# Layer 0 of a four-layer graph network: the pad term goes to one lane of four, and GpSimd clears the other three

## The chip, the core and the metric

The kernel runs on one core of a Trainium2 chip. The metric is the device time of one execution in microseconds (us), compared as a median of runs.

## The reference, cut to what matters

Four graph layers run over 128 graphs of 128 nodes with 64 features. Only layer 0 is touched. `F` is 64 and the hidden width `H` is 192.

```python
h = jnp.maximum(_layernorm(x, axis=-1), 0.0)
mask = (adj > 0.0).astype(x.dtype)
xj_proj = h @ W1a
diff = h[:, :, None, :] - h[:, None, :, :]
e = jax.nn.relu(xj_proj[:, :, None, :] + diff @ W1b + b1)
hm = jnp.einsum('bjkh,bjk->bjh', e, mask)
deg = jnp.sum(mask, axis=-1)
x = x + hm @ W2 + deg[..., None] * b2
```

For each node, a relu of (a term of the node) + (a term of the neighbour) is summed over the node's neighbours, and the sum goes through `W2`.

## The kernel before, in words

The rewritten sum needs two rows per node, made by one product per graph (`pe_ac`, L509): `A`, the node's own term, and `C`, the neighbour's. ScalarE copies them out as `ac32` (float32, L690) and `ac_hi` (float16, L691), and GpSimd makes the rest `ac_lo = ac32 - ac_hi` (`pool_low`, L883).

A node's neighbours are gathered slot by slot. In each of 8 slots of a chunk, a one-hot matrix (VectorE, `dve_onehot`, L811) picks one neighbour for every node, and TensorE adds the picked `C` row to the seeded `A` row in a PSUM bank (`pe_half`, `pe_next_half`, L551). Four slots are a half, 128 x 768 numbers wide. VectorE takes the negative part of each half and adds it to `acc`, a sum with four lanes of 192 (`dve_half`, L829). Later chunks do not start again: VectorE subtracts the old one-hot from the new one (`dve_difference`, L823) and TensorE adds that difference. In the trace each graph has two chunks, so four executions of L829. Nodes with many neighbours keep three more shared slots (`dve_shared_onehot`, L817, for the one-hot; `act_shared`, L708, to cut them).

Empty slots of a node add a known amount. That is the pad term, a relu of `A` times a negative factor `neg_pad` (per node, L781). `act_pads` (L699) starts `acc` with it: it writes a quarter of the term to each of the four lanes, so that VectorE's first L829 can add to it. After the last L829 of a graph, GpSimd folds the lanes, first four to two (`pool_sum`, L897), then the shared slots (L899, L901), and TensorE transposes and adds what is left (`pe_transpose_sum`, L523 to L528).

All five engines walk the same 128 steps, one graph a step, each with its own instruction order written out by hand and semaphores between them. A group is four steps, here called q = 0 to 3, and the preparation of the next group is spread over them: in q = 1 VectorE works out slot counts (L745 to L781), in q = 2 the first rows (L786 to L794), in q = 3 `dve_past_last` (L799, four instructions) and `dve_host_rows` (L805), for which `pe_host_ranks` (L494) waits. `acc`, `ac32`, `ac_hi` and `ac_lo` have four buffers, one for each q.

In step b, VectorE first waits for `s_acc0` (the start value of `acc`), then loops over the later chunks (one here), then does the two last halves with L817 between them. GpSimd in the same step, as soon as L823 is done, folds the graph before (L897, L899, L901), then makes `ac_lo` of the graph two ahead (L883), and then waits for the next L823:

```python
def step(b, g, u, q, nxt, p, use):
    if not (known(b) and b + 2 >= B):
        pool_low(pool, b + 2, (q + 2) % GS)
    pool_sum(pool, b, g, q, total, first)
```

ScalarE in step b cuts the shared slots of graph b - 1 (L708), seeds the second half of graph b (L715), copies `A` and `C` of graph b + 2 (L690, L691), and writes the start value of graph b + 1 (L699).

Of the kernel before, what the change touches and what calls it, by code (L numbers as in the profile page):

```python
# [7 lines left out]
ALU = mybir.AluOpType  # L8
ACT = mybir.ActivationFunctionType
# [3 lines left out]
def gnn_stack_kernel(nc, a, out):  # L13
# [12 lines left out]
    B, N, F = a["x"].shape  # L26
    H = a["L0_gnn_W2"].shape[0]
    D1 = a["L1_gnn_W0"].shape[1]
    GS = 4
    NG = B // GS  # L30
    NI = NG // 2
    SU = 4
    SC = 2 * SU
    SS = 3
# [14 lines left out]
    with ctx:  # L49
        def sb(name, shape, dt=F32):  # L50
            return ctx.enter_context(nc.sbuf_tensor(name, shape, dt))

        def sem(name):
            return ctx.enter_context(nc.semaphore(name))
# [94 lines left out]
        pad = sb("pad", [N, GS])  # L149
# [4 lines left out]
        neg_pad = sb("neg_pad", [N, 2, GS])  # L154
        h0 = sb("h0", [N, GS * F])
        hT0 = sb("hT0", [F + 1, 2, GS * N])
        ac32 = sb("ac32", [N, 4, 2 * H])
        ac_hi = sb("ac_hi", [N, 4, 2 * H], F16)
        ac_lo = sb("ac_lo", [N, 4, 2 * H], F16)
        acc = sb("acc", [N, 4, SU * H])  # L160
# [235 lines left out]
        s_rows = sem("rows_per_candidate_made")  # L396
        s_sum = sem("rows_per_candidate_summed")
        s_nop = sem("slot_count_step")
        s_n = sem("slot_counts_ready")
        s_st = sem("first_host_rows_made")  # L400
        s_first = sem("first_host_rows_copied")
# [23 lines left out]
        s_T = sem("sum_transposed")  # L425
# [13 lines left out]
        def known(v):  # L439
            return isinstance(v, int)  # L440
# [174 lines left out]
        def all_iterations(eng, body, prefetch_back_edge=False):  # L615
            around(0, body)
            with nc.Fori(1, NI - 1, engines=bass.OrderedEngineSet([eng.engine]),
                         hint_back_edge=prefetch_back_edge) as i:
                around(i, body)
            around(NI - 1, body)  # L620

        def group_of(b, g, u, q, back):

            r = q - back
            if 0 <= r < GS:
                return g, u, r
            return (g - 1, 1 - u, r + GS) if r < 0 else (g + 1, 1 - u, r - GS)
# [65 lines left out]
        def act_pads(act, b, g, p, q):  # L693

            act.wait_ge(s_n, g + 1)
            act.wait_ge(s_hi, b + 1)
            if not (known(b) and b < 4):
                act.wait_ge(s_hm, b - 3)
            nc.scalar.activation(acc[:, q, :].rearrange("p (t h) -> p t h", t=SU),  # L699
                                 ac32[:, q, 0:H].unsqueeze(1).broadcast_to([N, SU, H]), ACT.Relu,  # L700
                                 scale=neg_pad[:, p, q:q + 1]).then_inc(s_acc0, 1)

        def act_shared(act, b, q):
# [64 lines left out]
        def dve_pieces(dve, g, p):  # L768

            v = nc.vector  # L770
            dve.wait_ge(s_nop, 12 * g + 8)
            v.tensor_scalar(left_i[:, :], left[:, :], float(SS - 1), float(DIV), ALU.max, ALU.mult).then_inc(s_nop, 1)
            dve.wait_ge(s_nop, 12 * g + 9)
            v.tensor_scalar(pieces_i[:, :], left_i[:, :], SH, None, ALU.arith_shift_right).then_inc(s_nop, 1)
            dve.wait_ge(s_nop, 12 * g + 10)
            v.tensor_copy(pieces[:, :], pieces_i[:, :])
            v.scalar_tensor_tensor(out=pad[:, :], in0=pieces_i[:, :], scalar=-float(SS), in1=left[:, :],
                                   op0=ALU.mult, op1=ALU.add).then_inc(s_nop, 1)
            dve.wait_ge(s_nop, 12 * g + 11)

            v.tensor_scalar(neg_pad[:, p, :], pad[:, :], -float(SS - 1), 1.0 / SU, ALU.add, ALU.mult).then_inc(s_n, 1)  # L781

        def dve_first_rows(dve, g, p):
            dve.wait_ge(s_st, g + 1)
# [22 lines left out]
        def dve_onehot(dve, ranks, key, pos):  # L807

            dve.reg_alu(pos, pos, CH, ALU.bitwise_xor)
            at = dve.snap(pos, min_val=0, max_val=CH)  # L810
            nc.vector.tensor_scalar(onehot[:, ds(at, CH)], ranks.rearrange("p t j -> p (t j)"),  # L811
                                    slot_key[:, ds(key, 1)], None, ALU.is_equal).then_inc(s_G, 1)

        def dve_shared_onehot(dve, g, u, q):

            dve.wait_ge(s_rs2, g + 1)
            nc.vector.tensor_scalar(onehot2, rs2[:, u, q, :, :].rearrange("p t j -> p (t j)"),  # L817
                                    slot_key[:, 0:1], None, ALU.is_equal).then_inc(s_G2, 1)

        def dve_difference(dve, pos, old):  # L820

            at, at_old = (dve.snap(r, min_val=0, max_val=CH) for r in (pos, old))
            nc.vector.tensor_tensor(onediff[:, ds(at, CH)], onehot[:, ds(at, CH)], onehot[:, ds(at_old, CH)],  # L823
                                    ALU.subtract).then_inc(s_D, 1)

        def dve_half(k, q):

            sums = acc[:, q, :].rearrange("p (t h) -> p t h", t=SU)
            nc.vector.scalar_tensor_tensor(out=sums, in0=unit((q + k) % 2, 0, SU), scalar=0.0, in1=sums,  # L829
                                           op0=ALU.min, op1=ALU.add).then_inc(s_free[k], 1)  # L830

        def dve_slots(dve, b, g, u, q, regs, halfway, middle, beside, summed, late):
            cnt, prev, pos, old, count_reg = regs
            n = dve.snap(count_reg, min_val=1, max_val=NC + 1)
            dve.wait_ge(s_acc0, b + 1)
            dve.reg_mov(prev, cnt)
            dve.reg_add(cnt, cnt, 1)
            with dve.Fori(0, n) as c:
                dve.reg_mov(old, pos)
                dve_onehot(dve, rs[:, u, q, :, :], c + 1, pos)  # L840
                dve.reg_mov(prev, cnt)
                dve.reg_add(cnt, cnt, 1)
                dve.wait_ge(s_G, cnt)
                dve_difference(dve, pos, old)
                dve.wait_ge(s_done[0], prev)
                dve_half(0, q)
                dve.wait_ge(s_done[1], prev)
                dve.wait_ge(s_free[0], prev)
                dve_half(1, q)
            if not (known(b) and b == B - 1):  # L850
                g1, p1, q1 = group_of(b, g, u, q, -1)
                dve.wait_ge(s_n, g1 + 1)
                dve.reg_load(count_reg, chunks[0:1, ds(b + 1, 1)])
            halfway()
            dve.wait_ge(s_done[0], cnt)
            dve.wait_ge(s_free[1], prev)
            dve_half(0, q)
            middle()
            dve_shared_onehot(dve, g, u, q)
            beside()  # L860
            dve.wait_ge(s_done[1], cnt)
            dve.wait_ge(s_free[0], cnt)
            dve_half(1, q)
            summed()
            if not (known(b) and b == B - 1):
                dve.wait_ge(s_rs, g1 + 1)
                dve_onehot(dve, rs[:, p1, q1, :, :], 0, pos)
            late()
# [12 lines left out]
        def pool_low(pool, b, q):  # L881
            pool.wait_ge(s_hi, b + 1)
            nc.gpsimd.tensor_tensor(ac_lo[:, q, :], ac32[:, q, :], ac_hi[:, q, :], ALU.subtract)\  # L883
              .then_inc(s_lo, 1)

        def pool_sum(pool, b, g, q, total, first):
            pool.wait_ge(s_n, g + 1)
            n = pool.value_load(chunks[0:1, ds(b, 1)], min_val=1, max_val=NC + 1)
            pool.reg_add(total, total, n)
            pool.wait_ge(s_free2, b + 1)  # L890
            if not (known(b) and b == B - 1):
                pool.reg_add(first, total, 1)
                pool.wait_ge(s_D, first)
            else:
                pool.reg_add(first, total, B)
                pool.wait_ge(s_free[1], first)
            nc.gpsimd.tensor_tensor(acc[:, q, 0:2 * H], acc[:, q, 0:2 * H], acc[:, q, 2 * H:4 * H], ALU.add)  # L897
            shared = acc2[:, q % 2, :]
            nc.gpsimd.tensor_tensor(shared[:, 0:H], shared[:, 0:H], shared[:, H:2 * H], ALU.add).then_inc(s_half, 1)  # L899
            pool.wait_ge(s_half, b + 1)  # L900
            nc.gpsimd.tensor_tensor(hm2[:, q % 2, 0:H], shared[:, 0:H], shared[:, 2 * H:3 * H], ALU.add).then_inc(s_hm, 1)  # L901

        with nc.Block() as block:
# [179 lines left out]
            @block.gpsimd  # L1083
            def _(pool):
                total = pool.alloc_register("pool_differences")
                first = pool.alloc_register("pool_next_difference")
                pool.reg_mov(total, 0)
                pool_low(pool, 0, 0)
                pool_low(pool, 1, 1)

                def step(b, g, u, q, nxt, p, use):
                    if not (known(b) and b + 2 >= B):
                        pool_low(pool, b + 2, (q + 2) % GS)
                    pool_sum(pool, b, g, q, total, first)

                all_iterations(pool, step)
# [604 lines left out]
```

## Time and profile before

| | |
|---|---|
| median of 3 runs | 1501.34 us (1501.23 to 1503.02) |
| the profiled execution | 1501.28 us |
| its span, first to last instruction | 1499.6 us |
| mean granted TensorE clock | 0.968 |
| TensorE matmul busy | 1331.5 us (89%) |
| VectorE busy | 1172.1 us (78%) |
| ScalarE busy | 1112.1 us (74%) |
| GpSimd busy | 495.7 us (33%) |

The shares are averages over four layers with different limits. Layer 0 runs from about 52 us to 1034 us of the span, so what the change does is read from that stage.

### The profile page before, as it was taken

To read this page: it belongs to the slowest core of one execution; us is meant where nothing else is said; L and a number is where in the kernel's file an instruction comes from. 1 tells how busy PE (TensorE), PEld (TensorE's weight loads), DVE (VectorE), ACT (ScalarE), POOL (GpSimd) and SP (SyncE) were. 2 spreads that over 40 slices of the span, in tenths; PEclk is the share of its full clock that TensorE was granted. 3 is DMA by queue.
4 is the path that set the end of the run, shared out by engine and by line. 5 is a ranking of instruction groups with operands and counts; after the bars stand their busy time and mean duration, and the time that the engine had idled before them with its cause. 6 is when DMAs were issued, how large, how long until landed. Compare 5 with 4: busy or idle time off the path is not lost. (4 is left out here: it accounts for less than half of the span.)

```text
span 1499.6 us, 41694 instructions
## 1 busy us (share of the span) xinstructions
PE 1331.5 (89%) x11307; PEld 1084.8 (72%) x11308; DVE 1172.1 (78%) x3088; ACT 1112.1 (74%) x2424; POOL 495.7 (33%) x611
## 2 busy tenths in 40 slices
PE   0799999999999999999999999997999997881498
PEld 0577777777777777777777777775889987810498
DVE  6598898988988889889898898885444446968655
ACT  0788888888888888888888888873555555726675
POOL 0143344444444334333444444432111110076300
PEclk9999999999999999999999999998999998976699
DMA  7000000000000000000000000000000000000022
GB/s 148 15 9 9 15 7 7 7 14 7 7 7 10 11 7 7 7 14 7 7 7 14 7 7 7 0 2 1 1 0 0 0 0 0 0 1 0 11 49 52
DMA packets 40749, 18.08 MB, mean 12 GB/s; under 512 B 19396, under 2 KB 40710, under 8 KB 40710
## 3 DMA queue, kind: packets, MB, share of 16 engines
q1 hardware_dynamic: 40178, 17.39, 4.7%
q8 instruction: 19, 0.31, 0.1%
q10 hardware_dynamic: 532, 0.21, 0.1%
q14 instruction: 20, 0.16, 0.0%
HBM read 13.40 MB, written 4.19 MB: 12 GB/s over the span
## 5 line engine op out<-in xcount | busy, mean ns | idle before, releaser
L829 DVE SCALAR_TENSOR_TENSOR acc<-slot_banks,acc 128x768 f32<-128x768 f32 x512 | 486.8, 951 | 44.0 <-PE slot_banks L551 34.0
L897 POOL TENSOR_TENSOR acc<-acc 128x384 f32<-128x384 f32 x128 | 128.1, 1001 | 565.4 <-DVE onediff L823 560.9
L551 PE MATMUL slot_banks<-ac_hi,work 128*128 128x192 f16 x1408 | 264.4, 246 | 1.0 <-ACT slot_banks L715 1.0
L551 PE MATMUL slot_banks<-ac_lo,work 128*128 128x192 f16 x1408 | 263.9, 246 | 0.0
L551 PE MATMUL slot_banks<-ac_hi,onediff 128*128 128x192 f16 x1024 | 186.9, 248 | 20.8 <-DVE acc L829 16.9
L551 PE MATMUL slot_banks<-ac_lo,onediff 128*128 128x192 f16 x1024 | 185.8, 246 | 0.0
L551 PEld LDWEIGHTS slot_banks<-ac_hi,work 128*128 (+1 forms) x1408 | 137.3, 98 | 62.5 <-issue 43.4
L551 PEld LDWEIGHTS slot_banks<-ac_lo,work 128*128 (+1 forms) x1408 | 138.0, 98 | 14.9 <-issue 6.3
L811 DVE TENSOR_SCALAR work<-work,slot_key 128x1024 f16 x256 | 119.6, 478 | 28.6 <-issue 28.6
L551 PEld LDWEIGHTS slot_banks<-ac_hi,onediff 128*128 x1024 | 104.2, 102 | 43.2 <-issue 39.8
L708 ACT ACTIVATE work<-slot_banks 128x576 f32<-128x576 f32 x128 | 83.2, 650 | 68.6 <-PE slot_banks L551 68.6
L883 POOL TENSOR_TENSOR ac_lo<-ac,ac_hi 128x384 f16<-128x384 f32 x128 | 117.3, 916 | 48.1 <-ACT ac_hi L691 48.1
L651 ACT ACTIVATE work<-bank 128x512 f16<-128x512 f32 x256 | 130.5, 601 | 0.0
L699 ACT ACTIVATE acc<-ac,neg_pad 128x768 f32<-128x768 f32 x128 | 119.3, 932 | 0.0
L509 PE MATMUL bank<-wac,hT 65*128 65x384 f32 x256 | 109.2, 509 | 4.1 <-ACT ac_hi L691 4.1
L715 ACT ACTIVATE slot_banks<-ac 128x768 f32<-128x768 f32 x127 | 103.5, 815 | 11.6
L823 DVE TENSOR_TENSOR onediff<-work x128 | 88.6, 692 | 24.5 <-DVE work L811 24.5
L551 PEld LDWEIGHTS slot_banks<-ac_lo,onediff 128*128 x1024 | 100.7, 98 | 0.0
L1204 POOL TENSOR_TENSOR adjT_all<-adjT_all,ident 128x512 f32 x32 | 39.9, 1268 | 173.1 <-PE slot_banks L1158 173.1
L1125 ACT ACTIVATE onediff<-x_all,nmr,rstd 128x64 f32 (+1 forms) x256 | 90.6, 429 | 7.7 <-PE slot_banks L1295 3.2
L544 PE MATMUL slot_banks<-ac_hi,ident 128*128 128x384 f16 x258 | 84.6, 328 | 9.0 <-issue 7.8
L266 DVE BATCH_NORM_STATS2 bn<-x_all 128x6 f32<-128x64 f32 (+1 forms) x512 | 83.9, 212 | 8.0 <-DMA x_all<-in_x_dram 7.5
(254 smaller groups left out, 3330.3 us busy)
## 6 DMA issues: line engine op xcount, KB each, us to landing
adj_in<-in_adj_dram SPq DMA_DIRECT2D x32, 256.0 KB, 2.8
out_dram<-acc SPq DMA_DIRECT2D x32, 128.0 KB, 2.0
l1w<-in_L_gnn_W_dram SPq DMA_DIRECT2D x2, 64.0 KB
l1b<-in_L_gnn_b_dram SPq DMA_DIRECT2D x2, 64.0 KB
x_all<-in_x_dram SPq DMA_DIRECT2D x4, 0.2 KB, 12.0
nm_in<-in_nodemask_dram ACTq DMA_DIRECT2D x1, 64.0 KB
w1a<-in_L_gnn_W_dram ACTq DMA_DIRECT2D x1, 48.0 KB
w1b<-in_L_gnn_W_dram ACTq DMA_DIRECT2D x1, 48.0 KB
```

The source lines that it names most:

```text
L509: nc.tensor.matmul(pAC[:, 0:2 * H], hT0[:, p, q * N:(q + 1) * N], wac[:, :], start=True, stop=True)\
L544: nc.tensor.matmul(unit(pair, t, n), node, part[:, q, 0:H].unsqueeze(1).broadcast_to([N, n, H]), start=(e == 0), stop=False)
L551: last = nc.tensor.matmul(unit(pair, t, 1), hot(t), part[:, q, H:2 * H].unsqueeze(1), start=False, stop=(e == 1 and (t % SB == SB - 1 or t ...
L651: last = nc.scalar.activation(rs[:, p, :, t, :], pA3[:, :].rearrange("p (q j) -> p q j", q=GS), ACT.Copy, bias=-float(t))
L699: nc.scalar.activation(acc[:, q, :].rearrange("p (t h) -> p t h", t=SU), ac32[:, q, 0:H].unsqueeze(1).broadcast_to([N, SU, H]), ACT.Relu, ...
L715: nc.scalar.activation(unit((q + 1) % 2, 0, SU), ac32[:, q, 0:H].unsqueeze(1).broadcast_to([N, SU, H]), ACT.Copy).then_inc(s_seed, 1)
L811: nc.vector.tensor_scalar(onehot[:, ds(at, CH)], ranks.rearrange("p t j -> p (t j)"), slot_key[:, ds(key, 1)], None, ALU.is_equal).then_in ...
L823: nc.vector.tensor_tensor(onediff[:, ds(at, CH)], onehot[:, ds(at, CH)], onehot[:, ds(at_old, CH)], ALU.subtract).then_inc(s_D, 1)
L829: nc.vector.scalar_tensor_tensor(out=sums, in0=unit((q + k) % 2, 0, SU), scalar=0.0, in1=sums, op0=ALU.min, op1=ALU.add).then_inc(s_free[k ...
L883: nc.gpsimd.tensor_tensor(ac_lo[:, q, :], ac32[:, q, :], ac_hi[:, q, :], ALU.subtract)\
L897: nc.gpsimd.tensor_tensor(acc[:, q, 0:2 * H], acc[:, q, 0:2 * H], acc[:, q, 2 * H:4 * H], ALU.add)
L1125: ins = nc.scalar.activation(hn[:, u, SLOT[q] * F:(SLOT[q] + 1) * F], x[:, ds((b + q) * F, F)], ACT.Relu, bias=nmr[:, ds(b + q, 1)], scale ...
```

## The change

ScalarE's L699 writes the whole pad term to lane 0 alone, 128 x 192 numbers in place of 128 x 768, and `neg_pad` loses its factor of a quarter. GpSimd sets the three other lanes to zero with a new memset (`pool_clear`), one for each graph, placed behind `pool_low` in GpSimd's step. GpSimd first waits until the sum that last used the buffer was transposed, and VectorE waits for the memset (`s_zero`) beside `s_acc0`.

```diff
@@ act_pads
-            nc.scalar.activation(acc[:, q, :].rearrange("p (t h) -> p t h", t=SU),
-                                 ac32[:, q, 0:H].unsqueeze(1).broadcast_to([N, SU, H]), ACT.Relu,
+            nc.scalar.activation(acc[:, q, 0:H], ac32[:, q, 0:H], ACT.Relu,
                                  scale=neg_pad[:, p, q:q + 1]).then_inc(s_acc0, 1)
@@ dve_pieces
-            v.tensor_scalar(neg_pad[:, p, :], pad[:, :], -float(SS - 1), 1.0 / SU, ALU.add, ALU.mult).then_inc(s_n, 1)
+            v.tensor_scalar(neg_pad[:, p, :], pad[:, :], -float(SS - 1), None, ALU.add).then_inc(s_n, 1)
@@ dve_slots
             dve.wait_ge(s_acc0, b + 1)
+            dve.wait_ge(s_zero, b + 1)
@@ new
+        def pool_clear(q):
+
+            nc.gpsimd.memset(acc[:, q, H:SU * H], 0.0).then_inc(s_zero, 1)
@@ gpsimd
                 pool.reg_mov(total, 0)
+                pool_clear(0)
                 pool_low(pool, 0, 0)
...
                 def step(b, g, u, q, nxt, p, use):
+                    if not (known(b) and (b < 3 or b + 1 >= B)):
+                        pool.wait_ge(s_T, b - 2)
                     if not (known(b) and b + 2 >= B):
                         pool_low(pool, b + 2, (q + 2) % GS)
+                    if not (known(b) and b + 1 >= B):
+                        pool_clear((q + 1) % GS)
                     pool_sum(pool, b, g, q, total, first)
```

## Rows read from the trace of the kernel before

**Rows 1.** One stretch: us, busy PE PEld DVE ACT POOL (count), clock, DMA.
```profile
100.00:1000.00 900.00, 866.22 (x7925) 699.09 (x7923) 803.41 (x1980) 774.95 (x1590) 357.38 (x472) 1.00 0.03 8
```

**Rows 2.** Who waited for whom, 100 to 1000 us: total, times, longest.
```profile
ACT work L708 <- PE slot_banks L551: 63.3, 117, 1.0
DVE acc L829 <- PE slot_banks L551: 27.0, 75, 0.7
PE slot_banks L551 <- DVE acc L829: 16.3, 31, 2.5
PEld slot_banks L544 <- DVE acc L829: 15.3, 29, 0.8
PEld bank L494 <- issue: 7.0, 29, 0.3
```

**Rows 3.** Instructions of VectorE in order of time: start, length, idle before.
```profile
403.70 0.31 DVE L817 TENSOR_SCALAR work<-work,slot_key 128x384 f16<-128x384 f16 x1
...
406.66 0.48 DVE L811 TENSOR_SCALAR work<-work,slot_key 128x1024 f16 x1 [0.41 <-issue]
...
411.22 0.31 DVE L817 TENSOR_SCALAR work<-work,slot_key 128x384 f16<-128x384 f16 x1
...
412.71 0.73 DVE L794 TENSOR_SCALAR host<-row,start 128x128 f16<-128x128 f16 x4
...
415.77 0.96 DVE L829 SCALAR_TENSOR_TENSOR acc<-slot_banks,acc 128x768 f32<-128x768 f32 x1 [0.19 <-PE slot_banks L551]
...
418.33 0.40 DVE L805 TENSOR_TENSOR host<-host,work 128x512 f16<-128x512 f16 x1
418.65 0.94 DVE L829 SCALAR_TENSOR_TENSOR acc<-slot_banks,acc 128x768 f32<-128x768 f32 x1
```

**Rows 4.** TensorE in order of time, in the same two steps.
```profile
409.15 0.25 PE L551 MATMUL slot_banks<-ac_hi,onediff 128*128 128x192 f16 x1 [0.46 <-DVE acc L829]
...
418.83 0.38 PE L494 MATMUL bank<-row_slots,ones 128*128 128x512 f16 x1
...
419.74 0.32 PE L544 MATMUL slot_banks<-ac_hi,host 128*128 128x384 f16 x1
```

**Rows 5.** Groups by line, 100 to 1000 us: busy, mean ns of one, idle before.
```profile
L699 ACT ACTIVATE acc<-ac,neg_pad 128x768 f32<-128x768 f32 x118 | 110.0, 932 | 0.0
L720 ACT ACTIVATE hmTa<-bank,unscale 128x128 f32<-128x128 f32 x119 | 43.7, 367 | 12.9 <-PE bank L528 12.5
L799 DVE TENSOR_SCALAR work<-row,end 128x128 f16<-128x128 f16 x120 | 45.5, 439 | 0.0
L794 DVE TENSOR_SCALAR host<-row,start 128x128 f16<-128x128 f16 x120 | 22.0, 246 | 0.0
L817 DVE TENSOR_SCALAR work<-work,slot_key 128x384 f16<-128x384 f16 x117 | 36.0, 308 | 0.0
```

**Rows 6.** GpSimd's memsets, whole span: busy, mean ns of one.
```profile
L1199 POOL MEMSET onediff<- 128x896 f32 x1 | 0.8, 845 | 0.0
...
L298 POOL MEMSET hm<- 128x128 f32 x1 | 0.2, 204 | 0.0
```

**Rows 7.** VectorE and GpSimd around L799 in one q = 3 step.
```profile
417.00 0.95 DVE L799 TENSOR_SCALAR work<-row,end 128x128 f16<-128x128 f16 x1
...
416.98 0.91 POOL L883 TENSOR_TENSOR ac_lo<-ac,ac_hi 128x384 f16<-128x384 f32 x1
```

**Rows 8.** GpSimd in order of time, q = 1 and q = 2 of that group.
```profile
402.74 0.92 POOL L883 TENSOR_TENSOR ac_lo<-ac,ac_hi 128x384 f16<-128x384 f32 x1
408.11 1.00 POOL L897 TENSOR_TENSOR acc<-acc 128x384 f32<-128x384 f32 x1 [4.45 <-DVE onediff L823]
...
410.29 0.91 POOL L883 TENSOR_TENSOR ac_lo<-ac,ac_hi 128x384 f16<-128x384 f32 x1
```

**Rows 9.** VectorE's register and semaphore instructions, 400 to 432 us: ns min/median/max.
```profile
L834 DVEq FUSED_REGOPS  x3: 51/58/58, 406.1 to 429.1; - x3
...
L856 DVEq EVENT_SEMAPHORE  x4: 21/21/21, 402.5 to 425.7; - x4
```

More of the change, by code:

```diff
@@ L398, in gnn_stack_kernel @@
         s_nop = sem("slot_count_step")
+        s_zero = sem("sum_lanes_cleared")
         s_n = sem("slot_counts_ready")
```

## The prediction, written before the change was run

> **What bounds the kernel now.** I read the table of stretches first. In 900 us of layer 0, TensorE is busy for 866, VectorE for 803, ScalarE for 775 and GpSimd for 357 [rows 1]. So two engines are near their limit, and the change takes work from a third. Whether that third one ever holds anybody up is told by the list of waits: ScalarE's L708 stands idle 117 times for TensorE, 63.3 us in all, nearly once in each of the 118 steps there [rows 2]. So ScalarE is early in every step, and no wait for its start value (L699) is in the list. TensorE and VectorE wait for each other instead: VectorE's L829 for gathers, 27.0 us, TensorE's L551 and L544 for L829, 16.3 and 15.3 us [rows 2].
>
> Then I read the order of time, to see which of the two leads in which step. In q = 1 VectorE runs from L817 at 403.70 to L811 at 406.66 without idling for TensorE; only in front of that L811 stand 0.41 us in which it handles register and wait instructions [rows 3]. TensorE is behind it there: at 409.15 it has waited 0.46 us for L829 [rows 4]. In q = 2 the lead passes to TensorE: L829 at 415.77 has waited 0.19 us for it [rows 3]. In q = 3 it comes back: L805 ends at 418.73 and TensorE's L494, which needs it, starts at 418.83; L829 ends at 419.59 and L544, which needs that, starts at 419.74 [rows 3, 4]; TensorE's weight loads stood idle before L494 in 29 groups, 7.0 us [rows 2]. So a delay of VectorE in q = 1 or q = 3 is a delay of the whole group, and one in q = 2 is one beyond the first 0.19 us.
>
> **Removed: three quarters of L699.** It takes 932 ns for 768 columns; the nearest small ScalarE row, 128 columns, takes 367 [rows 5]. On the line between them 192 columns are about 0.42 us, an estimate, so about 0.51 us of each step goes, 65 us of ScalarE's time over 128 steps. On the path it gives nothing: L708 waits for TensorE afterwards as it did before, only longer [rows 2]. The dropped factor in L781 changes the operation's constants and not its shape of 128x4: nothing.
>
> **Added on GpSimd: one memset a step.** 128 columns took 204 ns, 896 took 845 [rows 6], so 576 columns are 204 + 448 x 0.835 = 578 ns. Its place is right behind L883. GpSimd then has time: it stands idle 4.45 us before the next L897 [rows 8]; were that cover gone, each step's fold would be 0.58 us later. Its own wait, for a transpose of two steps earlier, is met long before; behind it stand L883, the memset and the next fold, all inside that idle time. The result is in time for VectorE as well: behind the L883 that ends at 411.20 [rows 8] it is there at about 411.8, and VectorE first writes that buffer behind the L794 that start at 412.71 [rows 3].
>
> **Added on VectorE: one more wait a step.** The nearest rows are 21 ns for a semaphore instruction and 51 to 58 for one of registers [rows 9]. I take 0.07 us, bounds 0.02 and 0.14. It is hidden wherever VectorE's queue runs ahead of its datapath, and exposed where the 0.41 us gap stands, which is in front of two of four steps, one of them in [rows 3]: 0.14 us a group.
>
> **What the memset meets: the main term.** L799 and L794 are the same operation on the same shape, yet L799 takes 439 ns in the mean and L794 246 [rows 5]. The order of time shows why [rows 7]: one L799 starts at 417.00, beside GpSimd's L883, which started at 416.98, and both end together, L883 at 417.89 and L799 at 417.95. So this kind of VectorE instruction (TENSOR_SCALAR, float16, SBUF to SBUF) stands still while a GpSimd instruction that began before it runs. L817 and L811 are of that kind. L817 now never pays: its mean is 308 ns [rows 5], since it follows L883's end by a hair, 403.70 after 403.66 and 411.22 after 411.20 [rows 3, 8]. The memset fills exactly that place.
>
> The Trainium skill, SBUF — State Buffer, section Who interferes with whom, says that VectorE in a two-port mode and GpSimd lock each other out of a shared port pair for a whole instruction. By that rule the sum is the one below; [rows 7] agree for a GpSimd instruction that reads and writes, and no row of this trace shows it for a memset, which only writes.
>
> How much, in us, with the memset until 0.54 after L883's end (0.58 less the 0.04 that GpSimd's instructions overlap):
> - q = 1: L817 is released at 404.20. L799's end came 0.05 after the release; L817 has 256 columns more, at 0.24 ns each by the means of L794 and L817 [rows 5], so it ends 0.11 after: 404.31, not 404.01: **+0.30**, all on the path.
> - q = 2: the same, 411.85, not 411.53: +0.32. TensorE does not wait for this, so 0.19 is absorbed for VectorE; but GpSimd starts its next fold after L823, and so is 0.32 late in q = 3.
> - q = 3: four L799 stand there. The second is held by L883 as before, 0.32 later. The third followed it at the pace of four L794, (0.73 - 0.246) / 3 = 0.16 [rows 3, 5], so it ended at 418.11; now the memset holds it until 417.89 + 0.54 + 0.05 = 418.48, **+0.37**. Together **+0.69** for L805 and L829, for which TensorE waits.
> - q = 0: L817 comes well after L883 in some groups; 0 to 0.1, taken as 0.
>
> A group costs 0.30 + 0.69 + 0.14 = 1.13 us. Times 32 groups: 36 us. From the profiled 1501.28 (1499.6 of span and 1.7 around it, 0.06 under the median of the runs) that is **1537 us**. Below: if half of the delays fall into slack that the one group shown does not show, 1520. Above: if every one of q = 1 to 3 loses the whole 0.58, and L805 as well, 1.9 us a group and 1562.
>
> **Rivals.**
> - *Order saves L817.* Only 0.02 to 0.04 us lie between L883's end and L817's start. If L817 comes first, the memset waits and costs nobody; what stays is q = 3 (0.37) and the wait (0.14), 0.51 x 32 = 16: 1518 us. Against it: GpSimd's next instruction stands ready, and L883 got ahead of the second L799 by 0.02 us [rows 7]. The Trainium skill, SBUF — State Buffer, section Who interferes with whom, says that the one that issues first gets the pair; by that rule this rival hangs on those hundredths, and no row here shows a memset in such a race.
> - *A memset holds nobody.* It reads nothing, and the trace has no memset beside such a VectorE instruction. Then the wait alone is left: 0.14 x 32 = 4.5, 1506 us.
> - *Nothing on the path.* That wait too is hidden: 1501 to 1504 us.
> - *Faster.* ScalarE's 0.51 us comes through to TensorE's second half, which needs L715, behind L708. It decides only if L708 waits for ScalarE and not for TensorE, against 117 of 118 rows [rows 2]. TensorE's idle time in the stretch is 900 - 866 = 34 us, of which 31.6 are waits for L829 [rows 1, 2]; a third of 34 is the most I would give it: 1490 us.
>
> **How the numbers follow.** Main case 0.62 (its own range 1520 to 1562), order saves L817 0.14, memset holds nobody 0.13, nothing on the path 0.07, faster 0.04. A measurement here tells 0.2%, 3 us, from no change. Slower: 0.62 + 0.14 + 0.11 = 0.87; same: 0.07 + 0.02 = 0.09; faster 0.04. The range 1504 to 1552 keeps the first three but for the upper tail of the main case.
>
> **What would show it.** L817's mean above 308 ns, near 600 in q = 1 and q = 2; L799's mean above 439; L811 and L829 unchanged. L699 near 0.42 us and L708's wait longer by about 0.5 a step; a memset of 0.58 behind each L883. The gap before L811 0.48 in place of 0.41. L817 still at 308 would make the main term wrong; a shorter wait of L708 would make the faster rival right.

## The result, and the profile after

The changed kernel took 1530.35 us (median of 4 runs, 1527.87 to 1531.44), the kernel before 1501.81 beside it: a ratio of 1.0188, 95% interval 1.0173 to 1.0203. It is 28.5 us slower, where 35.7 were forecast. The profiled execution took 1531.44 us, its span 1529.7. TensorE's granted clock is 1.00 (its 2.4 GHz level) from 100 to 1000 us in both traces, so the clock is no part of the difference there.

In the changed kernel the numbers of the lines move: L699 is L700, L883 is L884, the fold L897 to L901 is L902 to L906, L551 is L552; the new memset is L889. VectorE's lines up to L829 keep theirs.

The groups by line, 100 to 1000 us, of the changed kernel (busy, mean ns of one, idle before), VectorE, ScalarE, GpSimd:

```profile
L829 DVE SCALAR_TENSOR_TENSOR acc<-slot_banks,acc 128x768 f32<-128x768 f32 x459 | 435.9, 950 | 33.0 <-PE slot_banks L552 22.3
L811 DVE TENSOR_SCALAR work<-work,slot_key 128x1024 f16 x230 | 107.9, 477 | 29.2 <-issue 29.2
...
L799 DVE TENSOR_SCALAR work<-row,end 128x128 f16<-128x128 f16 x116 | 52.8, 741 | 0.0
L817 DVE TENSOR_SCALAR work<-work,slot_key 128x384 f16<-128x384 f16 x115 | 50.9, 443 | 0.0
...
L700 ACT ACTIVATE acc<-ac,neg_pad 128x192 f32<-128x192 f32 x114 | 51.5, 452 | 0.0
...
L889 POOL MEMSET acc<- 128x576 f32 x115 | 66.7, 580 | 0.0
```

Two lines of the kernel before, same stretch, that [rows 5] does not have:

```profile
L829 DVE SCALAR_TENSOR_TENSOR acc<-slot_banks,acc 128x768 f32<-128x768 f32 x472 | 448.7, 951 | 36.4 <-PE slot_banks L551 27.0
L811 DVE TENSOR_SCALAR work<-work,slot_key 128x1024 f16 x236 | 110.5, 478 | 26.8 <-issue 26.8
```

Against [rows 5], L817 went from 308 to 443 ns in the mean and L799 from 439 to 741 (rows that are held together overlap, so L799's busy time grew less, from 45.5 us in 120 rows to 52.8 in 116); L811 and L829 kept their lengths. ScalarE's instruction shrank from 932 to 452. Where the time of ScalarE went is in the list of waits, same stretch:

```profile
ACT work L708 <- PE slot_banks L552: 67.0, 115, 1.0
ACT hmTa L720 <- PE bank L529: 56.2, 101, 1.2
...
DVE acc L829 <- PE slot_banks L552: 22.3, 57, 0.7
...
PE slot_banks L552 <- DVE acc L829: 20.5, 29, 0.9
```

ScalarE's wait at L720 grew from 12.5 us [rows 5] to 56.2, while that at L708 is about what it was, 63.3 us before [rows 2] and 67.0 now. TensorE's L552 waits a little longer for VectorE than in [rows 2]. The order of time shows the collision. VectorE and GpSimd, steps q = 1 and q = 2 of one group:

```profile
414.64 0.48 DVE L817 TENSOR_SCALAR work<-work,slot_key 128x384 f16<-128x384 f16 x1
...
417.83 0.49 DVE L811 TENSOR_SCALAR work<-work,slot_key 128x1024 f16 x1 [0.48 <-issue]
...
422.39 0.61 DVE L817 TENSOR_SCALAR work<-work,slot_key 128x384 f16<-128x384 f16 x1
```
```profile
413.58 0.92 POOL L884 TENSOR_TENSOR ac_lo<-ac,ac_hi 128x384 f16<-128x384 f32 x1
414.44 0.58 POOL L889 MEMSET acc<- 128x576 f32 x1
...
421.46 0.91 POOL L884 TENSOR_TENSOR ac_lo<-ac,ac_hi 128x384 f16<-128x384 f32 x1
422.31 0.58 POOL L889 MEMSET acc<- 128x576 f32 x1
```

In q = 2 the memset runs from 422.31 to 422.89 and L817, begun at 422.39, ends at 423.00, 0.11 us behind it; in [rows 3] the same instruction took 0.31. This is no single case: in all 56 steps with q = 1 or q = 2 between step 8 and step 119, L817 ends 0.11 to 0.12 us behind the memset. And q = 3, narrow windows that cut out single instructions, VectorE above, GpSimd below:

```profile
428.46 1.47 DVE L799 TENSOR_SCALAR work<-row,end 128x128 f16<-128x128 f16 x1
...
429.33 0.67 DVE L799 TENSOR_SCALAR work<-row,end 128x128 f16<-128x128 f16 x2
```
```profile
428.45 0.92 POOL L884 TENSOR_TENSOR ac_lo<-ac,ac_hi 128x384 f16<-128x384 f32 x1
...
429.30 0.58 POOL L889 MEMSET acc<- 128x576 f32 x1
```

The second L799 is not done until both GpSimd instructions are, 1.47 us after its start, at 429.93; the third and the fourth are done by 430.00.

### The profile page after: what moved, and what is told of

Read it like the earlier page. It is cut to its first block and busy times, and to the rows that moved or that the text cites. A ratio compares the mean times of both kernels' runs of the same rounds, so it can differ in the third digit from the quotient of the medians.

```text
span 1529.7 us, 41989 instructions
## 1 busy us (share of the span) xinstructions
PE 1342.9 (88%) x11307; PEld 1084.7 (71%) x11308; DVE 1197.2 (78%) x3088; ACT 1059.2 (69%) x2424; POOL 562.1 (37%) x739
## 5 line engine op out<-in xcount | busy, mean ns | idle before, releaser
L829 DVE SCALAR_TENSOR_TENSOR acc<-slot_banks,acc 128x768 f32<-128x768 f32 x512 | 486.3, 950 | 40.6 <-PE slot_banks L552 29.0
L902 POOL TENSOR_TENSOR acc<-acc 128x384 f32<-128x384 f32 x128 | 128.1, 1001 | 529.1 <-DVE onediff L823 524.6
L552 PE MATMUL slot_banks<-ac_hi,work 128*128 128x192 f16 x1408 | 264.4, 246 | 1.0 <-ACT slot_banks L715 1.0
L552 PE MATMUL slot_banks<-ac_lo,work 128*128 128x192 f16 x1408 | 263.8, 246 | 0.0
L552 PE MATMUL slot_banks<-ac_hi,onediff 128*128 128x192 f16 x1024 | 188.0, 247 | 28.5 <-DVE acc L829 22.7
L552 PE MATMUL slot_banks<-ac_lo,onediff 128*128 128x192 f16 x1024 | 186.7, 246 | 0.0
L552 PEld LDWEIGHTS slot_banks<-ac_hi,work 128*128 (+1 forms) x1408 | 137.4, 98 | 53.2 <-issue 34.2
L552 PEld LDWEIGHTS slot_banks<-ac_lo,work 128*128 (+1 forms) x1408 | 138.1, 98 | 20.2 <-issue 7.2
L811 DVE TENSOR_SCALAR work<-work,slot_key 128x1024 f16 x256 | 119.9, 477 | 32.3 <-issue 32.3
L552 PEld LDWEIGHTS slot_banks<-ac_hi,onediff 128*128 x1024 | 103.4, 101 | 53.8 <-issue 48.3
L708 ACT ACTIVATE work<-slot_banks 128x576 f32<-128x576 f32 x128 | 83.4, 651 | 76.6 <-PE slot_banks L552 76.6
L884 POOL TENSOR_TENSOR ac_lo<-ac,ac_hi 128x384 f16<-128x384 f32 x128 | 117.4, 917 | 30.8 <-ACT ac_hi L692 30.8
L720 ACT ACTIVATE hmTa<-bank,unscale 128x128 f32<-128x128 f32 x128 | 47.1, 368 | 77.6 <-PE bank L529 77.3
L552 PEld LDWEIGHTS slot_banks<-ac_lo,onediff 128*128 x1024 | 100.5, 98 | 0.0
L691 ACT ACTIVATE ac<-bank 128x384 f32<-128x384 f32 x128 | 62.3, 486 | 46.1 <-PE bank L510 46.0
```

The costliest lines, as they stand in the source:

```text
L552: last = nc.tensor.matmul(unit(pair, t, 1), hot(t), part[:, q, H:2 * H].unsqueeze(1), start=False, stop=(e == 1 and (t % SB == SB - 1 or t ...
L708: nc.scalar.activation(acc2[:, q % 2, :].rearrange("p (t h) -> p t h", t=SS), unit(q % 2, 0, SS), ACT.Relu, scale=-1.0).then_inc(s_free2, 1)
```

## The experiments

Theory A: the memset holds back VectorE's float16 TENSOR_SCALAR instructions, and VectorE leads in these steps. Theory B: the cost is VectorE's new dependence on GpSimd, the wait and what hangs on it. A third, that ScalarE's shorter instruction changes the time, was left in for both signs.

The measure that told most is the length of a step, from the first L829 of one step to the first of the next, in us, worked out from the starts of L829 in each trace as a mean over steps 8 to 119 (28 of each q):

| kernel | q = 0 | q = 1 | q = 2 | q = 3 | group | median us | ratio to before, 95% interval |
|---|---|---|---|---|---|---|---|
| before | 7.960 | 7.559 | 6.757 | 8.158 | 30.434 | 1501.81 | |
| the changed kernel | 8.034 | 7.948 | 6.987 | 8.423 | 31.392 | 1530.35 | 1.0188 (1.0173 to 1.0203) |
| e1 memset behind L817 | 7.928 | 7.930 | 7.103 | 8.451 | 31.412 | 1531.51 | 1.0190 (1.0157 to 1.0223) |
| e2 wait only | 8.027 | 7.758 | 6.683 | 8.160 | 30.628 | 1508.08 | 1.0036 (1.0021 to 1.0051) |
| e3 lane 0 only | 7.960 | 7.554 | 6.757 | 8.156 | 30.427 | 1499.42 | 0.9978 (0.9963 to 0.9993) |
| e4 short memset | 8.027 | 7.758 | 6.683 | 8.156 | 30.624 | 1510.55 | 1.0036 (1.0020 to 1.0051) |
| e5 full in q = 1 | 8.031 | 7.950 | 6.688 | 8.159 | 30.828 | 1514.21 | 1.0080 (1.0057 to 1.0103) |
| e6 full in q = 2 | 8.031 | 7.761 | 6.989 | 8.163 | 30.944 | 1517.30 | 1.0100 (1.0070 to 1.0129) |
| e7 full in q = 3 | 8.031 | 7.761 | 6.688 | 8.419 | 30.899 | 1514.34 | 1.0080 (1.0051 to 1.0109) |
| e8 second memset | 8.244 | 8.354 | 7.393 | 8.830 | 32.821 | 1575.99 | 1.0490 (1.0460 to 1.0521) |
| e9 memset before pool_low | 8.129 | 7.770 | 6.782 | 7.756 | 30.437 | 1498.44 | 0.9976 (0.9962 to 0.9989) |
| e10 before, pool_low late in q = 3 | 7.958 | 7.555 | 6.755 | 7.447 | 29.715 | 1482.24 | 0.9865 (0.9847 to 0.9884) |

The medians are over all runs. The ratios are those on record; they differ from the quotients of the medians by up to 0.0013 (e2, e3). The kernel before was run beside each set, with medians of 1504.62 beside e1 to e4, 1502.07 beside e5 to e8 and 1502.73 beside e9 and e10. e5 to e8 have two or three runs each; for them the lengths of the steps tell more than the medians.

**e1: the memset only when L817 is done.**

```diff
             pool.wait_ge(s_n, g + 1)
+            last = known(b) and b + 1 >= B
+            if not last and True:
+                pool.wait_ge(s_G2, b + 1)
             n = pool.value_load(chunks[0:1, ds(b, 1)], min_val=1, max_val=NC + 1)
             pool.reg_add(total, total, n)
+            if not last:
+                pool_clear((q + 1) % GS)
             pool.wait_ge(s_free2, b + 1)
...
-                    if not (known(b) and b + 1 >= B):
-                        pool_clear((q + 1) % GS)
```

> The changed kernel with one edit: GpSimd starts each memset only when L817 of the same step is done, so that it runs beside L829, which reads PSUM and one SBUF tensor. Same memset, same extra wait of VectorE, same ScalarE. Theory A (the memset holds back VectorE's float16 TENSOR_SCALAR instructions): L817 back to a mean of 308 ns and the four L799 to 439, and the time falls to that of the kernel before plus the wait's share, 0.07 us in two steps of four and up to 0.13 more in one place: 1504 to 1509 us. Theory B (the cost is the new dependence of VectorE on GpSimd, or GpSimd's added work as such): nothing changes, 1527 to 1533 us.

1531.51 us, as slow as the change, which theory A had not expected. The groups of e1 by line tell why:

```profile
L811 DVE TENSOR_SCALAR work<-work,slot_key 128x1024 f16 x230 | 144.9, 630 | 37.7 <-issue 37.7
...
L799 DVE TENSOR_SCALAR work<-row,end 128x128 f16<-128x128 f16 x116 | 45.1, 448 | 0.0
L817 DVE TENSOR_SCALAR work<-work,slot_key 128x384 f16<-128x384 f16 x115 | 35.4, 308 | 0.0
```

L817 and L799 are back where theory A put them, and L811, one more of their kind, has gone from 478 to 630 ns. One place of it, VectorE and then GpSimd:

```profile
422.04 0.31 DVE L817 TENSOR_SCALAR work<-work,slot_key 128x384 f16<-128x384 f16 x1
422.27 0.95 DVE L829 SCALAR_TENSOR_TENSOR acc<-slot_banks,acc 128x768 f32<-128x768 f32 x1
423.13 0.90 DVE L811 TENSOR_SCALAR work<-work,slot_key 128x1024 f16 x1
```
```profile
423.18 0.58 POOL L889 MEMSET acc<- 128x576 f32 x1 [1.16 <-DVE work L817]
```

L817 ends at 422.35, but the memset starts 0.83 us later, since GpSimd loads a register between the wait and the memset. So it ran beside the end of L829 only, and met L811. The loop's body holds eight steps, two groups. In seven of them L811 starts between 0.05 us ahead of the memset and 0.24 us behind its start, is held, and ends 0.28 us behind its end. In the eighth L811 starts about 0.15 us ahead, keeps its length, and it is the memset that takes longer, 0.83 us in the mean. One such place, VectorE and then GpSimd:

```profile
407.60 0.47 DVE L811 TENSOR_SCALAR work<-work,slot_key 128x1024 f16 x1
```
```profile
407.74 0.85 POOL L889 MEMSET acc<- 128x576 f32 x1 [1.16 <-DVE work L817]
```

The victim changed and the cost stayed: the instruction that is held follows the memset, which speaks for A, but the time lies where B put it, and the run alone does not refute B.

**e2: one more wait of VectorE, and nothing else.**

```diff
             dve.wait_ge(s_acc0, b + 1)
+            dve.wait_ge(s_lo, b + 1)
```

> The kernel before with one more wait of VectorE at the start of each step, on a GpSimd result that is always long there (L883 of two steps earlier). No memset, ScalarE as before. Theory A: the gap in front of L811 grows from 0.41 to 0.48 us in two steps of four, 0.14 us a group, and nothing else: 1505 to 1508 us. Theory B (the wait is the main cost): 1520 us or more. If the wait is hidden: 1502 us.

1508.08 us, ratio 1.0036. A group is 0.194 us longer, 6.2 us over 32 groups, where A expected 0.14: a fifth of the change's cost. The bare wait falls as the main cause; what else B could mean is left to e4.

**e3: ScalarE's part alone.**

```diff
-            dve.wait_ge(s_zero, b + 1)
+            if known(b) and b == 0:
+                dve.wait_ge(s_zero, GS)
...
-                pool_clear(0)
+                for r in range(GS):
+                    pool_clear(r)
...
-                    if not (known(b) and (b < 3 or b + 1 >= B)):
-                        pool.wait_ge(s_T, b - 2)
...
-                    if not (known(b) and b + 1 >= B):
-                        pool_clear((q + 1) % GS)
```

> The changed kernel without the memset of each step and without VectorE's wait for it; the three lanes are cleared once at the start and then keep what they held, so the sums are not the reference's. What is left is ScalarE's shorter L699. Theory A: ScalarE only waits longer at L708, 1501 to 1503 us. The rival that ScalarE's relief helps: under 1498 us, with L708 waiting less than 63 us in 100 to 1000 us. The rival that a changed rhythm of ScalarE costs: over 1505 us.

1499.42 us, a little under the expected 1501 to 1503, ratio 0.9978. Yet a group is 30.427 us long against 30.434: ScalarE's relief is worth nothing in the steps that repeat. Laid beside the kernel before step by step, 1.9 of the 3.1 us by which layer 0's stretch of L829 is shorter fall at step 120, the first one behind the loop: it takes 8.86 us in place of 10.79. ScalarE is not alone in moving that step, which takes 10.07 in e2, where ScalarE is as before; the cause is open.

**e4: the same memset, but one lane.**

```diff
-            nc.gpsimd.memset(acc[:, q, H:SU * H], 0.0).then_inc(s_zero, 1)
+            nc.gpsimd.memset(acc[:, q, H:2 * H], 0.0).then_inc(s_zero, 1)
...
+                for r in range(GS):
+                    nc.gpsimd.memset(acc[:, r, 2 * H:SU * H], 0.0)
                 pool_clear(0)
```

> The changed kernel with a memset of one lane in place of three, 192 columns, about 0.26 us by its line of 0.835 ns a column; the other two lanes are cleared once at the start and then keep what they held, so the sums are not the reference's. Same place, same waits, same number of instructions. Theory A: the memset ends 0.22 us after L884, before L817 or the last L799 would have ended on their own; L817 at most 340 ns and L799 at most 480 in the mean, 1504 to 1511 us. Theory B (a memset in this place, or its semaphore, costs whatever its length): 1525 us or more.

1510.55 us, ratio 1.0036, and its four steps are those of e2 within 0.004 us. L817 is at 308 ns; L799 at 495, a little over the 480 that A allowed, but its four rows overlap more and take no longer together than in e2. One place in q = 2, VectorE and then GpSimd:

```profile
413.19 0.31 DVE L817 TENSOR_SCALAR work<-work,slot_key 128x384 f16<-128x384 f16 x1
```
```profile
413.11 0.26 POOL L889 MEMSET acc<- 128x192 f32 x1
```

L817 starts while the short memset runs, and yet takes its 0.31 us: it ends at 413.50, 0.13 behind the memset, which is later than the 0.11 to which the full memset holds it. So a memset in the same place, with the same waits, costs nothing when it is over 0.11 us before L817 would end anyway, and B falls. What is left over e2's wait is therefore the length of the memset: 31.392 - 30.624 = 0.768 us a group, 24.6 us over 32 groups.

**e5, e6, e7: the full memset in one step of four.**

```diff
-        def pool_clear(q):
-
-            nc.gpsimd.memset(acc[:, q, H:SU * H], 0.0).then_inc(s_zero, 1)
+        def pool_clear(q, lanes=1):
+
+            nc.gpsimd.memset(acc[:, q, H:(1 + lanes) * H], 0.0).then_inc(s_zero, 1)
...
-                        pool_clear((q + 1) % GS)
+                        pool_clear((q + 1) % GS, 3 if q == 1 else 1)
```

(`q == 1` stands for e5, 2 for e6, 3 for e7; 3 and 1 are numbers of lanes cleared. As in e4 the other lanes are cleared once at the start.)

> The kernel of the short memset (one lane of 192 columns in every step; the other lanes cleared once at the start, so the sums are not the reference's), but in step q = 1 the memset is the full one of 576 columns. Theory A: only L817 of q = 1 gets longer, by 0.17 to 0.25 us, and the step q = 1 with it; 0.19 x 32 = 6 us over the kernel of the short memset, 8 to 10 by the size of the prediction. The rival that TensorE's lead absorbs it: under 2 us.

> As the one before, with the full memset in step q = 2 alone. Theory A: L817 of q = 2 gets longer by 0.30 us; of that 0.09 is VectorE's former wait for TensorE in q = 3, but GpSimd is later too and holds the first L799 longer, so 0.3 x 32 = 10 us over the kernel of the short memset. The rival that TensorE's lead in q = 2 absorbs it: under 5 us.

> As the one before, with the full memset in step q = 3 alone. Theory A: the last L799 ends 0.63 us after L884 in place of 0.38, 0.25 x 32 = 8 us over the kernel of the short memset (0.37 x 32 = 12 by the size of the prediction). If theory A holds for all three, their sum over the kernel of the short memset is the 24 us by which the changed kernel is longer than that one.

Over e4 a group grew by 0.204, 0.320 and 0.275 us, 0.799 together against the 0.768 of all three at once. Each cost stands in its own step of the table, and no step's cost is absorbed by TensorE. In e6 VectorE's former wait for TensorE in q = 3 did take up 0.09, and GpSimd's being late gave it back at L799, whose four rows last 1.56 us from the first start to the last end, in place of 1.47 in e4. By the medians, each against the kernel before beside it, the three cost 6.2, 9.3 and 6.3 us more than e4, where 6, 10 and 8 were expected.

**e8: a longer hold.**

```diff
+        spare = place(896).bitcast(F32)
...
                         pool_clear((q + 1) % GS)
+                        nc.gpsimd.memset(spare, 0.0)
```

> The changed kernel with a second memset behind each first one, of 448 columns of unused memory, 0.47 us by its line. Theory A: L817 and the last L799 are held 0.47 us longer in q = 1, 2 and 3, and in q = 0 L817, which comes 0.31 us after L884 in every second group, is reached as well: 1.4 to 1.7 us a group, 1570 to 1585 us. The rival that a second instruction finds the lock taken by VectorE in between, so that only the first one costs: 1529 to 1540 us.

1575.99 us, as A expected. In this kernel L817 is L818:

```profile
L818 DVE TENSOR_SCALAR work<-work,slot_key 128x384 f16<-128x384 f16 x110 | 77.0, 700 | 0.0
...
L1105 POOL MEMSET work<- 128x448 f32 x110 | 51.9, 471 | 0.0
```

Every step pays: 0.41 us more than in the changed kernel in q = 1, 2 and 3, and 0.21 in q = 0, 1.43 a group. No held instruction of VectorE ended between the two memsets. The second one writes memory that nobody reads and signals no semaphore, so the hold does not come from a dependence of the program.

**e9: the whole change, with GpSimd's order turned round.**

```diff
             nc.gpsimd.tensor_tensor(shared[:, 0:H], shared[:, 0:H], shared[:, H:2 * H], ALU.add).then_inc(s_half, 1)
+            if not (known(b) and (b < 2 or b + 2 >= B)):
+                pool.wait_ge(s_T, b - 1)
             pool.wait_ge(s_half, b + 1)
...
-                    if not (known(b) and (b < 3 or b + 1 >= B)):
-                        pool.wait_ge(s_T, b - 2)
-                    if not (known(b) and b + 2 >= B):
-                        pool_low(pool, b + 2, (q + 2) % GS)
                     if not (known(b) and b + 1 >= B):
                         pool_clear((q + 1) % GS)
+                    if not (known(b) and b + 2 >= B):
+                        pool.wait_ge(s_G2, b + 1)
+                        pool_low(pool, b + 2, (q + 2) % GS)
```

> The whole change with GpSimd's order turned round: the memset stands right behind the fold (L901 of the kernel before), and the pool_low instruction waits until L817 of the step is done. In q = 0 to 2 the memset then runs beside L829 alone, and in q = 3 L799 is held by the memset, 0.58 us, in place of pool_low, 0.92. Theory A: L817 at 308 ns and L799 shorter than 439 in the mean; pool_low beside L829 may touch the next L811 by 0.1 to 0.2 us. The wait's 4 us stay, q = 3 gives back up to 0.3 a group: 1496 to 1510 us. Theory B (the memset costs wherever it stands): 1525 us or more.

1498.44 us: the same memset, the same extra wait of VectorE, ScalarE as changed, and the median is 4.3 us under that of the kernel before beside it, where the changed kernel was 28.5 above. A group is as long as in the kernel before, 30.437 against 30.434. L817 is at 308 ns again. In q = 0 to 2 the memset now runs beside L829, which keeps its 950 ns, so L829 is not held. In q = 3, L799 is held by the memset, 0.58 us, and no longer by pool_low, 0.92. Its mean of 573 ns is not under 439, as A had put it, because its rows overlap more; but its busy time falls from 45.5 us to 34.6 for the same 120, and the step from 8.158 to 7.756. This pays for VectorE's wait and for L811, which pool_low touches:

```profile
L811 DVE TENSOR_SCALAR work<-work,slot_key 128x1024 f16 x236 | 118.7, 513 | 30.2 <-issue 30.2
...
L817 DVE TENSOR_SCALAR work<-work,slot_key 128x384 f16<-128x384 f16 x118 | 36.3, 308 | 0.0
L799 DVE TENSOR_SCALAR work<-row,end 128x128 f16<-128x128 f16 x120 | 34.6, 573 | 0.0
```

**e10: the kernel before, with pool_low late in one step of four.** If A holds, the kernel before pays the same price already.

```diff
                     if not (known(b) and b + 2 >= B):
+                        if q == 3:
+                            pool.wait_ge(s_G2, b + 1)
                         pool_low(pool, b + 2, (q + 2) % GS)
```

> The kernel before with one edit: in step q = 3 GpSimd starts pool_low (L883) only when L817 of the step is done. No memset, no extra wait of VectorE, ScalarE as before. Theory A says that L883 already holds L799 in the kernel before, 0.7 us a group: L799 falls from 439 ns to 260 in the mean. VectorE gains up to 0.6 us in q = 3; TensorE idles only 0.24 us before L494 there, so 0.25 to 0.6 x 32: 1482 to 1494 us, faster than both kernels. If VectorE's float16 instructions are held by something else than GpSimd: 1501 us.

1482.24 us, ratio 0.9865 (0.9847 to 0.9884): faster than both kernels. From the groups and the waits of e10:

```profile
L799 DVE TENSOR_SCALAR work<-row,end 128x128 f16<-128x128 f16 x120 | 24.3, 262 | 0.0
```
```profile
POOL ac_lo L883 <- DVE work L817: 67.6, 30, 2.4
```

GpSimd waits 2.4 us at most in these 30 steps; L811, which L883 now touches there, goes from 478 to 489 ns in the mean. L799 falls to 262 ns, and q = 3 from 8.158 to 7.447 us. That is 0.71 a group, more than the 0.25 to 0.6 expected: the 0.24 us that TensorE idles before L494 cannot be all the slack that it has in that step.

## Why the prediction was right, step by step

**The main term was right in its mechanism.** A memset, which only writes, holds back L817 and L799 until it is over; a short one in the same place costs nothing (e4), a longer one more (e8), one elsewhere meets another of their kind (e1) or, in three steps of four, L829, which it does not hold (e9). The Trainium skill, SBUF — State Buffer, section Who interferes with whom, gives the rule for it, an exclusive port pair held for the whole instruction; the traces agree as to the hold, with L817 at 0.61 us beside a memset of 0.58 and at 0.31 without. That it is this port pair, and that L817 runs in a two-port mode, no trace shows. The rivals "order saves L817" and "a memset holds nobody" fall by the same rows.

**Its size was 0.22 us a group too large.** Forecast were 0.99, 0.30 in q = 1 and 0.69 for q = 2 and q = 3 together; the changed kernel pays 0.19, and 0.30 and 0.27, more than e4, with 0.01 in q = 0. Both places are too large by about the same, 0.11 and 0.12:
- q = 3: the text had the second L799 released by L883 and the third held by the memset, with the rest at a pace of 0.16: +0.37. In fact the second is held through both, and the two behind it end within 0.07 us of it, 0.035 apart: +0.27.
- q = 1: L817 stood 0.04 us behind L883 in [rows 3, 8], and stands 0.14 us behind L884 in the group above (414.64 after 414.50). In every second group it comes so much later and is held 0.1 less. The wait alone brings that shift: in e2, too, the second and third L829 of q = 1 start 1.34 us apart in the mean, in place of 1.29 before. The forecast took the two terms as independent; they are not.

**The wait was right in kind and 0.05 us too small.** Forecast 0.14 us a group, measured 0.194 (e2). The loop's body holds two copies of the group, and they pay differently: 0.13 in one and 0.26 in the other. In the first, the gap before the L811 of q = 1 grew by 0.14 more than the 0.07 forecast, but the q = 2 behind it became 0.15 shorter. In the second the gaps grew by 0.07 to 0.08, as forecast, and the rest lies between the second and the third L829 of q = 1, 1.40 us apart in place of 1.28. Why the copies differ is open, and nothing read from the trace of before told of it.

**ScalarE's relief is worth nothing in the steps that repeat**, as forecast: e3's groups are as long as those of before. Its L700 takes 452 ns, where the line between two rows gave 420. Where the removed 0.48 us of a step would show was forecast wrongly: L708 was to wait 0.5 us longer a step, but its sum went from 63.3 us to 67.0 only (69.3 in e3), and the wait came at L720, 12.5 to 56.2. The rival "faster" needed a shorter wait of L708; e3's 0.2% are no sign of it, since they lie outside the repeating steps.

The sum by the measured terms is (0.768 + 0.194) x 32 = 31 us, where 1.13 x 32 = 36 were forecast; the two errors partly cancel. The medians differ by 28.5, and layer 0's stretch of L829 grew by 28.7. Of these the 28 groups from step 8 to step 119 pay 26.8, the first two groups 1.8 and the last two 0.1; the forecast counted all 32 alike.

## What to carry to other kernels

Before work is moved to an engine that is two thirds idle, look at what its neighbour runs at the moment that it would fill: here GpSimd's idle time was no free time, because VectorE's float16 instructions stood exactly in it. Two instructions of one shape with different means, like L799 and L794, can be the sign of such a hold, and here a cheaper repair than moving work was to move the instruction that holds: one wait in one step of four gave 1.35%. And a wait that is to place an instruction should stand right in front of it: in e1 a register load between the two made the memset 0.83 us late.

## What the runs showed of the hardware that was not expected

- The end of a row tells of the hold, and not its start or its length. L817 ends 0.11 to 0.12 us behind the full memset, whether it started 0.01 or 0.17 behind L884's end; in e4 its row overlapped the short memset by up to 0.20 us and was not longer for it.
- The earlier start of a row does not say who goes first: in e1, L811 starts at 423.13 and the memset at 423.18, and yet L811 is the one held. Started 0.15 us ahead, it is not held, and the memset is. That L829 in front of it runs until 423.22 in the first place may be the reason; no run tests it.
- Held instructions pile up and end close together: three L799, whose starts stay 0.16 us apart when nothing holds them, ended within 0.07 us. The third one's row starts at 429.33, at L884's end, so by the starts alone VectorE would seem to have gone on between the two GpSimd instructions; none of the three ended before the memset did.
- One added wait cost 0.07 us in each of the two places where VectorE has no work queued, and in q = 1 up to 0.14 more, at different instructions in the two copies of the group in the loop's body. What makes the copies differ is open.
